# A second attention whose scores are x M x^T: one product a block goes, and the row maxima pass through GpSimd

## The reference

```python
qkv = einsum('btc,cd->btd', x, W) + b          # W: 128 x 384
q, k, v = split(qkv, 3)
weights = einsum('btc,bTc->btT', q, k) / sqrt(128)
logits = where(tril == 0, -9e15, weights)
values = einsum('btT,bTc->btc', softmax(logits), v)
```

## Time and the profile before

| what | value |
|---|---|
| three runs | median 724.75 us, 723.85 to 725.23 |
| span of the profiled execution | 722.4 us |
| TensorE products busy | 659.3 us (91%) |
| VectorE busy | 587.1 us (81%) |
| ScalarE busy | 486.4 us (67%) |
| GpSimd busy | 309.0 us (43%) |
| mean granted TensorE clock | 0.971 |

### The profile page before, as it was taken

The page is one execution under the profiler, slowest core; times in us unless marked ns, Lnnn a source line. Parts: engine busy times, 40 slices in busy tenths (PEclk is TensorE's granted clock), DMA queues, the critical chain, the costliest instruction groups (busy, mean ns, idle before and its releaser), DMA issues.

```text
span 722.4 us, 13085 instructions
## 1 busy us (share of the span) xinstructions
PE 659.3 (91%) x3654; PEld 508.6 (70%) x3654; DVE 587.1 (81%) x1873; ACT 486.4 (67%) x978; POOL 309.0 (43%) x793
## 2 busy tenths in 40 slices
PE   3466679999999999999999999999999999999994
PEld 2354557787878777777878787777868787767652
DVE  1566778989898898889898898889897998877672
ACT  2243548587786878686877877686877868676623
POOL 1234443445453535536454535436454535340311
PEclk9787979999999999999999999999999999999997
DMA  6000000000000010101000000101000000000001
GB/s 226 12 4 15 1 16 0 16 1 16 15 15 15 1 30 2 31 0 29 0 15 16 5 25 0 30 0 29 0 21 9 15 0 0 15 1 15 16 0 30
DMA packets 18678, 12.51 MB, mean 17 GB/s; under 512 B 704, under 2 KB 18240, under 8 KB 18368
## 3 DMA queue, kind: packets, MB, share of 16 engines
q1 hardware_dynamic: 18624, 11.95, 5.5%
HBM read 7.75 MB, written 4.19 MB: 17 GB/s over the span
## 4 chain that ended last, share of the span: by engine, by line
PE 68%; DVE 14%; ACT 7%; issue 6%; POOL 3%; DMA 1%; DVEq 0%; ACTq 0%; SPq 0%; POOLq 0%
PE bank L556 13%; PE bank L351 8%; PE bank L353 8%; PE bank L352 8%; PE bank L360 8%; PE bank L439 2%; PE bank L466 2%; PE bank L411 2%; PE bank L454 2%; DVE conv L954 2%; DVE gu L1067 1%; PE bank L477 1%; PE bank L510 1%; PE bank L478 1%; PE bank L523 1%
## 5 line engine op out<-in xcount | busy, mean ns | idle before, releaser
L556 PE MATMUL bank<-hid,whole 128*128 128x512 f32 x288 | 147.2, 593 | 0.8 <-DVE hid L1070 0.8
L351 PE MATMUL bank<-x3T_hi,w_hi 128*128 128x512 f32 x288 | 138.2, 480 | 1.8 <-DVE gu L1067 1.4
L738 ACT ACTIVATE silu<-bank 128x512 f32<-128x512 f32 x144 | 86.4, 600 | 65.0 <-PE bank L353 61.9
L1067 DVE TENSOR_TENSOR gu<-silu,bank 128x512 f32<-128x512 f32 x128 | 86.7, 677 | 41.1 <-ACT silu L738 18.5
L353 PE MATMUL bank<-x3T_hi,w_lo 128*128 128x512 f32 x288 | 113.5, 394 | 0.0
L352 PE MATMUL bank<-x3T_lo,w_hi 128*128 128x512 f32 x288 | 112.7, 391 | 0.0
L1171 POOL TENSOR_TENSOR moment<-stats 128x4 f32<-128x4 f32 x192 | 44.8, 266 | 150.1 <-DVE stats L881 134.3
L1077 DVE TENSOR_TENSOR hid<-gu,bank 128x512 f32<-128x512 f32 x128 | 87.2, 681 | 1.8 <-PE bank L556 0.8
L351 PEld LDWEIGHTS bank<-x3T_hi,w_hi 128*128 128x128 f32 x288 | 54.2, 188 | 31.0 <-ACT silu L738 9.9
L1157 POOL TENSOR_TENSOR qk<-rope_c,rope_s 128x512 f32<-128x512 f32 x32 | 40.6, 1280 | 82.6 <-DVE rope_s L843 82.6
L1171 POOL TENSOR_TENSOR rstd<-moment,whole 128x4 f32<-128x4 f32 x64 | 64.7, 1011 | 5.0
(11 more groups left out here) (196 smaller groups left out, 1635.7 us busy)
## 6 DMA issues: line engine op xcount, KB each, us to landing
x_in<-x SPq DMA_DIRECT2D x16, 256.0 KB, 2.9
out<-x SPq DMA_DIRECT2D x16, 256.0 KB, 2.3
whole<-w_whole SPq DMA_DIRECT2D x1, 1198.5 KB, 5.7
w_raw<-w SPq DMA_DIRECT2D x1, 1152.0 KB
w_raw<-w SPq DMA_DIRECT2D x1, 546.0 KB, 7.0
whole<-w_whole SPq DMA_DIRECT2D x16, 32.0 KB
whole<-w_whole SPq DMA_DIRECT2D x1, 64.0 KB
```

Source lines behind the costliest of these rows:

```text
L351: mm(out, wh, mh, start=True, stop=False)
L556: mm(YB[:], whole[:, a:a + P], hid[:, c % 2], start=c == 0, stop=c == CHUNKS).then_inc(p_w2.sem, 1)
L738: fn(silu[:, c % 2], GB[:], ACT.Silu).then_inc(a_silu.sem, 1)
L1067: tt(gu[:, c % 2], silu[:, c % 2], UB[:], ALU.mult).then_inc(v_gu.sem, 1)
```

## The change

The scores of a row pair are q k^T = (x Wq + bq)(x Wk + bk)^T. With M = Wq Wk^T and r = Wk bq this is x M x^T + (r x^T) + a term that depends on the query row alone, x Wq bk + bq bk. The softmax does not see a term that is constant along a row, but the change keeps it in the maxima by way of a column. In detail:

- In turn 0 each engine gets a piece at its end that folds the weights: TensorE transposes Wq and Wk, forms M, r, Wq bk and bq bk; ScalarE copies them out; VectorE prepares the rest.
- `c_project` makes one product, M with x. `ckT`, its product L478 and its copy L696 go; the scores take `xT[2]` in place of `ckT`.
- The value weights get a 129th column, Wq bk, so that the row term comes out as column 128 of `cv`. The values of two tiles go to B0 (ahead of the last `d_down`), of the other two to B1, and VectorE adds the bias in two halves.
- `c_max` writes plain maxima `top_s`. A new GpSimd piece `c_shift`, first in GpSimd's turn, adds the row column and subtracts again to give `neg_max`; `c_exp` waits for it.
- Both sequences' scores wait for their half of the value addition; `a_qT_` gets a wait for GpSimd's `qk`.
- The setup's scaled copy of the query bias goes. The order of the pieces that remain is as before.

```diff
 # TensorE
             def a_qT_(n):
                 pe.wait_ge(a_g.sem, a_g.at(n))
+                pe.wait_ge(g_qk.sem, g_qk.at(n))
...
+            def fold_keys():
+                nc.tensor.transpose(B0[:, 0:P], raw("cq"), ident)
+                nc.tensor.transpose(B0[:, P:2 * P], raw("ck"), ident).then_inc(p_fold.sem, 1)
+                pe.wait_ge(a_fold.sem, 1)
+                pe.wait_ge(v_fold.sem, 3)
+                wqT, wkT = foldT[:, 0:P], foldT[:, P:2 * P]
+                mm(B1[:, 0:P], wqT, wkT, start=True, stop=True)
+                mm(B1[:, P:P + 1], wkT, const("bcq"), start=True, stop=True)
+                mm(B1[:, P + 1:P + 2], wqT, const("bck"), start=True, stop=True)
+                mm(B1[:, P + 2:P + 3], const("ones"), b_qk[:], start=True, stop=True).then_inc(p_fold.sem, 1)
...
             def c_project(n):
+                if not started(n):
+                    pe.wait_ge(a_fold.sem, 5)
                 pe.wait_ge(a_xT[2].sem, a_xT[2].at(n))
-                mm(B1[:], raw("cq"), xT[2][:], start=True, stop=True).then_inc(p_cq.sem, 1)
-                mm(B0[:], raw("ck"), xT[2][:], start=True, stop=True).then_inc(p_ck.sem, 1)
-            def c_value(n):
-                pe.wait_ge(a_cq.sem, a_cq.at(n))
-                for t in range(TILES):
-                    last = mm(tile(B1, t), tile(xT[2], t), raw("cv"), start=True, stop=True)
+                mm(B1[:], m_qk[:], xT[2][:], start=True, stop=True).then_inc(p_cq.sem, 1)
+            def c_value(n, half):
+                if half == 1:
+                    pe.wait_ge(a_cq.sem, a_cq.at(n))
+                b = B1 if half else B0
+                for i in range(2):
+                    last = mm(b[:, i * SEQ:i * SEQ + CVW], tile(xT[2], 2 * half + i), w_cv[:], start=True, stop=True)
                 last.then_inc(p_cv.sem, 1)
             def c_scores(n):
-                pe.wait_ge(a_ck.sem, a_ck.at(n))
                 for s, b in ((0, B0), (1, B1)):
-                    if s == 1:
-                        pe.wait_ge(v_cv.sem, v_cv.at(n))
+                    pe.wait_ge(v_cv.sem, v_cv.at(n, s + 1))
                     q0, q1 = tile(cqT, 2 * s), tile(cqT, 2 * s + 1)
-                    k0, k1 = tile(ckT, 2 * s), tile(ckT, 2 * s + 1)
+                    k0, k1 = tile(xT[2], 2 * s), tile(xT[2], 2 * s + 1)
...
                 if b: c_project(i - 1)
+                if b: c_value(i - 1, 0)
                 if d: d_down(i - 3, 8)
-                if b: c_value(i - 1)
+                if b: c_value(i - 1, 1)
+                if first_turn(i): fold_keys()
 # ScalarE
+            def fold_keys():
+                act.wait_ge(p_fold.sem, 1)
+                fn(foldT[:], B0[:, 0:2 * P], ACT.Copy).then_inc(a_fold.sem, 1)
+                act.wait_ge(p_fold.sem, 2)
+                fn(m_qk[:], B1[:, 0:P], ACT.Copy, scale=C_SCALE).then_inc(a_fold.sem, 1)
...
-            def c_qkv(n):
+            def c_query(n):
                 act.wait_ge(p_cq.sem, p_cq.at(n))
-                fn(cqT[:], B1[:], ACT.Identity, scale=C_SCALE, bias=bcq_s[:]).then_inc(a_cq.sem, 1)
-                act.wait_ge(p_ck.sem, p_ck.at(n))
-                fn(ckT[:], B0[:], ACT.Identity, bias=const("bck")).then_inc(a_ck.sem, 1)
+                fn(cqT[:], B1[:], ACT.Identity, bias=r_b[:]).then_inc(a_cq.sem, 1)
             def c_exp(n):
                 for s, b in ((0, B0), (1, B1)):
-                    act.wait_ge(v_max.sem, v_max.at(n, 2 * s + 2))
+                    act.wait_ge(g_max.sem, g_max.at(n, 2 * s + 2))
 # VectorE
+            def fold_bias():
+                tt(b_qk[:], const("bcq"), const("bck"), ALU.mult).then_inc(v_fold.sem, 1)
+                nc.vector.tensor_copy(w_cv[:, 0:P], w_raw[:, WEIGHT_COLS["cv"][0]:WEIGHT_COLS["cv"][1]]).then_inc(v_fold.sem, 1)
+                nc.vector.tensor_copy(b_cv[:, 0:P], const("bcv")).then_inc(v_fold.sem, 1)
...
-                        red(neg_max[:, 2 * s + i:2 * s + i + 1], b[:, a:a + w], AX.X, ALU.max, negate=True).then_inc(v_max.sem, 1)
-            def c_value(n):
-                dve.wait_ge(p_cv.sem, p_cv.at(n))
-                tt(cv[:], tiles(B1[:]), const("bcv").unsqueeze(1).broadcast_to([P, TILES, P]), ALU.add).then_inc(v_cv.sem, 1)
+                        red(top_s[:, 2 * s + i:2 * s + i + 1], b[:, a:a + w], AX.X, ALU.max).then_inc(v_max.sem, 1)
+            def c_value(n, half):
+                dve.wait_ge(p_cv.sem, p_cv.at(n, half + 1))
+                tt(cv[:, 2 * half:2 * half + 2], by_tile(B1 if half else B0)[:, :, 0:CVW],
+                   b_cv[:].unsqueeze(1).broadcast_to([P, 2, CVW]), ALU.add).then_inc(v_cv.sem, 1)
 # GpSimd
+            def c_shift(n):
+                for s in range(SEQS):
+                    pair, row = slice(2 * s, 2 * s + 2), cv[:, 2 * s:2 * s + 2, P]
+                    pool.wait_ge(v_max.sem, v_max.at(n, 2 * s + 2))
+                    pool.wait_ge(v_cv.sem, v_cv.at(n, s + 1))
+                    tt(top_l[:, pair], top_s[:, pair], row, ALU.add).then_inc(g_max.sem, 1)
+                    pool.wait_ge(g_max.sem, g_max.at(n, 2 * s + 1))
+                    tt(neg_max[:, pair], row, top_l[:, pair], ALU.subtract).then_inc(g_max.sem, 1)
             def turn(i, odd):
+                if c: c_shift(i - 2)
                 if a: x0_lo(i)
```

More of the change, by code:

```diff
@@ L46 @@
 KV = P + HEADS
+CVW = P + 1
 LOGITS = PROJ + len(RANKS)
@@ L104, in second, with first_turn @@
     return isinstance(i, int) and i == 1
+def first_turn(i):
+    return isinstance(i, int) and i == 0
 def started(n):
@@ L178, in build @@
         b_logit = sb("b_logit", [P, LOGITS])
-        bcq_s = sb("bcq_s", [P, 1])
+        foldT = sb("foldT", [P, 2 * P])
+        m_qk = sb("m_qk", [P, P])
+        r_b = sb("r_b", [P, 1])
+        b_qk = sb("b_qk", [P, 1])
+        w_cv = sb("w_cv", [P, CVW])
+        b_cv = sb("b_cv", [P, CVW])
         x_in = sb("x_in", [P, 2, TILES, P])
@@ L234, in build @@
         cqT = sb("cqT", [P, BLOCK])
-        ckT = sb("ckT", [P, BLOCK])
-        cv = sb("cv", [P, TILES, P])
+        cv = sb("cv", [P, TILES, CVW])
+        top_s = sb("top_s", [P, TILES])
+        top_l = sb("top_l", [P, TILES])
         neg_max = sb("neg_max", [P, TILES])
@@ L297, in build @@
         a_small = sig("a_small")
-        p_cq, p_ck, p_cv, p_s, p_pT, p_av = sig("p_cq"), sig("p_ck"), sig("p_cv"), sig("p_s", 2), sig("p_pT", 2), sig("p_av")
-        a_cq, a_ck, v_cv, v_max, a_exp, a_pT, v_rinv = (sig("a_cq"), sig("a_ck"), sig("v_cv"), sig("v_max", 4),
-                                                        sig("a_exp", 4), sig("a_pT", 2), sig("v_rinv"))
+        p_cq, p_cv, p_s, p_pT, p_av = sig("p_cq"), sig("p_cv", 2), sig("p_s", 2), sig("p_pT", 2), sig("p_av")
+        a_cq, v_cv, v_max, g_max, a_exp, a_pT, v_rinv = (sig("a_cq"), sig("v_cv", 2), sig("v_max", 4), sig("g_max", 4),
+                                                         sig("a_exp", 4), sig("a_pT", 2), sig("v_rinv"))
+        p_fold, a_fold, v_fold = sig("p_fold"), sig("a_fold"), sig("v_fold")
         R_MASKED, R_TOP = 13, 17
@@ L374, in _ @@
             pe.wait_ge(setup_v.sem, 13)
-            pe.wait_ge(setup_a.sem, 4)
+            pe.wait_ge(setup_a.sem, 3)
             def a_xT_(n, half, load):
@@ L509, in c_av @@
                 for s in range(SEQS):
-                    mm(tile(B1, 2 * s), probT[:, s, 0:P], cv[:, 2 * s], start=True, stop=True)
-                    mm(tile(B1, 2 * s + 1), probT[:, s, P:2 * P], cv[:, 2 * s], start=True, stop=False)
-                    last = mm(tile(B1, 2 * s + 1), probT[:, s, 2 * P:3 * P], cv[:, 2 * s + 1], start=False, stop=True)
+                    mm(tile(B1, 2 * s), probT[:, s, 0:P], cv[:, 2 * s, 0:P], start=True, stop=True)
+                    mm(tile(B1, 2 * s + 1), probT[:, s, P:2 * P], cv[:, 2 * s, 0:P], start=True, stop=False)
+                    last = mm(tile(B1, 2 * s + 1), probT[:, s, 2 * P:3 * P], cv[:, 2 * s + 1, 0:P], start=False, stop=True)
                 last.then_inc(p_av.sem, 1)
@@ L621, in _ @@
             fn(escale[:], clamp_t[:], ACT.Exp).then_inc(setup_a.sem, 1)
-            fn(bcq_s[:], const("bcq"), ACT.Copy, scale=C_SCALE).then_inc(setup_a.sem, 1)
             fn(up_x[:], const("up", 3 * SUB), ACT.Copy).then_inc(setup_a.sem, 1)
@@ L625, in _ @@
             fn(w_hi[:, W_LATE:], w_raw[:, W_LATE:W_SPLIT], ACT.Copy).then_inc(setup_a.sem, 1)
-            act.wait_ge(setup_a.sem, 4)
+            act.wait_ge(setup_a.sem, 3)
             act.wait_ge(setup_v.sem, 13)
+            def fold_keys():
[3 more added lines that the diff above has]
+                fn(m_qk[:], B1[:, 0:P], ACT.Copy, scale=C_SCALE).then_inc(a_fold.sem, 1)
+                fn(r_b[:], B1[:, P:P + 1], ACT.Copy, scale=C_SCALE).then_inc(a_fold.sem, 1)
+                fn(w_cv[:, P:CVW], B1[:, P + 1:P + 2], ACT.Copy, scale=C_SCALE).then_inc(a_fold.sem, 1)
+                fn(b_cv[:, P:CVW], B1[:, P + 2:P + 3], ACT.Copy, scale=C_SCALE).then_inc(a_fold.sem, 1)
             def split_late():
@@ L690, in b_dnT @@
```

(32 more changed lines are left out.)

## The result

| | before | after |
|---|---|---|
| median of four runs beside each other, us | 724.99 (723.85 to 726.24) | 766.34 (766.19 to 767.51) |
| ratio, 95% interval | | 1.057 [1.0554, 1.0585] |
| span of the profiled execution, us | 722.4 | 764.4 |
| mean granted TensorE clock | 0.971 | 0.952 |

The kernel is 5.7% slower. Forecast were 752.9 us and a range up to 764; the direction and the hold behind `c_shift` came as said, the size did not.

The account below looks back on a forecast made before the run. TensorE, nearly gapless from 120 us, was taken as the bound. Terms 13.8 + 9.9 + 2.7 + 0.8 + 0.65 + 0.3 = 28.1 us on the 722.4 span, plus 2.35 carried over, gave 752.9 us; range 743 to 764.

Parts of the forecast that it names:

- the hold behind `c_shift`: On GpSimd, `x0_lo` waits behind `c_shift` for the second sequence's maxima, delaying TensorE's `a_vT_` by 1.72 us in an ordinary turn.
- ordinary turns: Turns 4, 5, 6, 7, 9, 11, 13, 15: `a_vT_` starts 1.72 us later, TensorE idles 2.3 us; 13.8 us in all.
- after the jump: Turns 8, 10, 12, 14, after the loop's jump: `a_vT_` +3.03 us, +2.47 net, TensorE idle 3.6 us; 9.9 us in all.
- The wait for `comb`: TensorE reaches the transposes of `comb` 0.86 us earlier but waits for VectorE; 0.29 us of the gain goes.
- the end of the wait for `probT`: TensorE's wait at `c_av` for `probT` goes, except in the last turns; 0.56 us returned in each turn after the jump.
- the last turns: Turns 16 and 17: `exp` 0.56 us later in both, removed product gains 0.86 once: +0.3 us.
- The small operations: `c_shift` on GpSimd: 0.20 us per operation, from the four-column row; chain from maxima 0.56 us, bounds 0 and 0.84.
- rival 2: TensorE's new idle halves its clock: 6 to 10 us more after the jump, 18 to 30 in twelve turns; chance 0.12.
- The sign that the prediction had set for this rival: For rival 2: waits as forecast, but TensorE's busy time grows at a granted clock under 1.00.
- the first turns: `a_vT_` later by 2.71 us in turn 3 and 0.83 in turn 2; turn 0's fold +0.65.
- The fold: Weight work at the end of turn 0 delays `x0T` of turn 1: +0.65 us, bounds 0 and 2.
- Rival 1: TensorE's gain stays, maxima in before GpSimd could begin `x0T_lo`: 12 turns gain 0.57 us each, 718.6 us; chance 0.06.

Follow-up runs that it names:

- the run that takes the clock out: Kernel after, with nine more 512-column products on TensorE in `a_vT_`, ahead of its wait for `x0T_lo`: 756.98 us, 1.0452 of before.
- the hold alone: Kernel before, with one wait added: GpSimd waits for the second sequence's maxima before `x0_lo`; 761.71 us, 1.0511 of before.

## Why the prediction was right and where it failed

**The hold came as worked out.** GpSimd held `x0T_lo` behind the maxima, and TensorE idled 2.04 to 2.20 us in ordinary turns (2.3 was said) and 3.08 to 3.32 after the jump (3.6). Ordinary turns at full clock grew by 1.50 to 1.96 us against the 1.72 of the sum (turn 3 to 4 is 41.54 us where it was 40.04; turn 6 to 7 is 41.68 for 39.72). In the run that takes the clock out, twelve turns lose 23.3 us; the sum had 23.6. The wait for `comb`, the end of the wait for `probT` but for the last turns, turn 2's 0.85 for 0.83, all stand.

**The small operations.** On two columns they take 0.20 and 0.19 us, as those on four did. The estimate of 0.06 us from the Trainium skill's page "GPSIMD Engine Reference", section 3.1, is not borne out at this size: the measurement decides. From the end of the second pair of maxima (153.91 + 0.62) to the start of `x0T_lo` (155.03) the kernel after takes 0.50 us, where 0.56 was taken: this term was sized well.

**The step that failed: the sum put the clock at nothing, and rival 2 was set aside for the ordinary turns.** The prediction found that their idle time "resembles the first" of the two stretches in the earlier trace rows, the one that kept 1.00; it took the clock into its upper end for the jump turns alone, and gave the rival a chance of 0.12. But all four jump turns fell to half clock, and three of eight ordinary ones did too, at 1.57 us each. The price named was 1.5 to 2.5; the 3 to 5 us of slow work behind it stood on no row. The sign that the prediction had set for this rival came: the waits were as said, and TensorE's busy time grew, at a clock of 0.98 from 120 to 700 us. For the first turns no clock term was worked out at all: from turn 2 to turn 3 they lost 5.83 us instead of 2.71. By TensorE's starts in the two timelines, the hold in turn 3 is 2.66 us of it (2.71 was said); 0.7 us go behind turn 2's hold, 1.6 at the eight products shown above and the wait ahead of them, and 0.9 ahead of `att`. The same instruction with the shift behind `x0_lo`:

```profile
85.65 1.17 PE L443 MATMUL bank<-kv_m,qT 128*128 128x136 f32 x8 [2.19 <-DVE kv_m L895]
```

That the clock makes these 3.1 us is read from the rows and not tested: in the early turns TensorE has other gaps, and the filler kept 1.00 behind turn 2's hold but ran at 0.50 from 90 to 108 us, and its turn 2 to 3 is 41.66 us, not much under the 42.15.

The Trainium skill, page "TensorE: Matmul & The Clock Gate", section "Why this matters for your kernels", warned that idle gaps between bursts put the clock back to half; the trace agrees in the jump turns. The ordinary turns' gaps are shorter than those that the section warns of, and three of eight lost the clock all the same.

**The account.** The span grew by 42.0 us, 13.9 more than the sum. Of these, 10.9 lie between turns 3 and 15 (34.58 measured, 23.64 in the sum), 3.1 between turns 2 and 3, 0.5 in turn 1, and the last turns give 0.7 back (-0.37 for +0.3). In time it is 13.4 us, since the median lay 1.9 us above the span and not the 2.35 that was carried over. The clock in the jump turns alone, 4 x 1.57 = 6.3 us, would have left the time inside the range, at about 759; the three ordinary turns (4.7) and the first turns (3.1) took it out.

**The fold was undersized.** It was put at 0.65 us, with bounds 0 and 2. Turn 1's `a_vT_` starts 1.11 us later (40.26, before 39.15), in an execution whose first transposes began 0.45 us earlier: 1.56. Its four products took 1.70 us in the kernel without a shift (35.39 to 37.09), where about 1.0 was taken. Moving it into the gaps returned 1.32 us of time.

**Rival 1 did not come, but another kernel comes near its number.** Without the shift, 3.5 to 4.4 us of the 6.2 that it worked out are gained: 720.8 us where it had 718.6, and 719.5 with the fold moved.

## What to carry to other kernels

Before putting a small piece at the head of an in-order engine, ask what it waits for and which ready piece stands behind it: here operations of 0.8 us a turn cost 45 us in all, and moving them one place back returned 35. A hold that opens an idle gap on TensorE has two prices, the gap and the clock behind it; when gaps of the new length have not been seen between full stretches, put half clock into the forecast for all of them. And first ask whether the piece is needed: a term that is constant along a row can be left out of the maxima altogether.

## What was not expected of the hardware

The same hold, 2.04 us of idle TensorE, left the clock at 1.00 in turn 4 and was followed by some 3 us at 0.50 in turn 5, in one execution. Turns 6, 9, 11 and 15, with holds of 2.12 to 2.20 us, kept the clock; turns 7 and 13, with 2.13 and 2.12, lost it. The run with the hold alone shows it at shorter ones: turns 6 and 13 lost the clock behind 1.84 and 1.76 us, and turns 7, 9, 11 and 15 kept it behind 1.76. So the length of the idle time alone does not decide it in this range, and what else does stays open: no run here was made to separate it. The four holds of 3.08 to 3.32 us all lost it.
